# State-space scan on one core: output product by chunk with sums of squares on its diagonal, decays two chunks ahead

## What is computed

```python
xn = _rmsnorm(x, norm_w, eps)                 # x: layer-normed tokens
zxbcdt = einsum('bld,ed->ble', xn, W_in)      # z 256, x|B|C 256+32+32, dt 8
xBC = silu(causal convolution of 4 taps over tokens + conv_b)
dt = softplus(dt + dt_bias); dA = exp(dt * -exp(A_log))
state = state * dA_t + (dt_t * x_t) B_t       # for every token, 8 heads of 32 x 32
y_t = state C_t
y = y + Dp * xs
y = _rmsnorm(y * silu(z), gnorm_w, 1e-05)     # mean over the 256 channels of y
return x + einsum('ble,de->bld', y, W_out)
```

## Time and profile before

| | us |
|---|---|
| median of 3 runs | 1113.69 |
| lowest and highest of them | 1113.39, 1123.93 |
| the profiled execution's own time | 1116.23 |
| its span, first to last instruction | 1114.4 |

### The profile page before, as it was taken

How to read it: one execution, slowest core, us unless ns; L and a number is a source line. 1 busy time by engine, 2 the same in 40 slices (tenths; PEclk the granted TensorE clock), 3 DMA queues, 4 the chain that set the end, 5 groups by cost and what they waited for, 6 DMA issues and landing times.

```text
span 1114.4 us, 20011 instructions
## 1 busy us (share of the span) xinstructions
PE 928.4 (83%) x7790; PEld 737.3 (66%) x7790; DVE 712.2 (64%) x1838; ACT 542.2 (49%) x859; POOL 236.8 (21%) x194
## 2 busy tenths in 40 slices
PE   3798899988986786878787797778979999999998
PEld 2554665556655575766676676667757878888877
DVE  2856776777662746364646446564566888878875
ACT  1534554444744653628273454626334455655453
POOL 0052001110104241414223141412532001111000
PEclk8899999999986778788878778787959999999999
DMA  5420000000002200203030200303010000000000
GB/s 148 153 114 19 19 20 2 19 20 20 1 9 57 49 19 15 52 2 65 1 67 1 47 20 8 60 1 66 7 53 1 20 1 20 20 20 20 20 1 39
DMA packets 30765, 36.16 MB, mean 32 GB/s; under 512 B 4560, under 2 KB 24784, under 8 KB 30672
## 3 DMA queue, kind: packets, MB, share of 16 engines
q1 hardware_dynamic: 29520, 30.68, 11.3%
q10 hardware_dynamic: 1152, 4.19, 1.0%
...
## 4 chain that ended last, share of the span: by engine, by line
PE 53%; DVE 28%; ACT 8%; issue 6%; POOL 2%; DMA 1%; SPq 1%; DVEq 0%; ACTq 0%; POOLq 0%
PE ps L1028 6%; DVE cacc L1682 6%; PE ps L684 5%; PE ps L947 4%; PE ps L763 3%; DVE acc L1959 3%; PE ps L765 3%; PE ps L764 3%; PE ps L671 3%; DVE nmax L1539 2%; PE ps L638 2%; ACT X L1234 2%; ACT un L1354 2%; PE ps L883 2%; PE ps L643 2%
## 5 line engine op out<-in xcount | busy, mean ns | idle before, releaser
L1773 DVE SCALAR_TENSOR_TENSOR dcy<-dcy,g_sb 128x1024 f32<-128x1024 f32 x64 | 95.4, 1491 | 117.9 <-ACT dcy L1310 117.5
L1959 DVE SCALAR_TENSOR_TENSOR acc<-ps,comb,acc 128x128 f32<-128x128 f32 x512 | 141.2, 344 | 21.5 <-PE ps L1028 20.6
L1028 PEld LDWEIGHTS ps<-w_f,hid 128*128 128x128 f32 x1024 | 131.2, 191 | 16.5 <-ACT hid L1373 8.2
L1028 PE MATMUL ps<-w_f,hid 128*128 128x128 f32 x1024 | 136.7, 277 | 4.8 <-ACT hid L1373 4.8
L1373 ACT ACTIVATE hid<-ps,b_f 128x512 f32<-128x512 f32 x128 | 86.3, 686 | 107.7 <-PE ps L765 107.4
L1310 ACT ACTIVATE dcy<-ps 128x1024 f32<-128x1024 f32 x64 | 65.4, 1021 | 134.9 <-PE ps L883 134.8
L1539 DVE TENSOR_REDUCE nmax<-ps 128x1 f32<-128x1024 f32 x64 | 78.1, 1221 | 39.7 <-PE ps L643 39.3
L518 POOL TENSOR_TENSOR xdt<-xs,dts 128x256 f32<-128x256 f32 x64 | 58.3, 913 | 211.6 <-PE ps L924 211.6
L1682 DVE SCALAR_TENSOR_TENSOR cacc<-ps,cw,cacc 128x1023 f32<-128x1023 f32 (+5 forms) x72 | 91.8, 1276 | 8.6 <-ACT cacc L1247 7.2
L1163 ACT ACTIVATE probs<-ps,nmax 128x1024 f32<-128x1024 f32 x64 | 71.3, 1114 | 41.3 <-DVE nmax L1539 38.4
L671 PEld LDWEIGHTS ps<-id_f,probs 128*128 128x128 f32 x512 | 60.0, 144 | 32.5 <-issue 22.9
...
## 6 DMA issues: line engine op xcount, KB each, us to landing
...
```

The lines of the kernel that those rows point to most:

```text
L1028: last = nc.tensor.matmul(ps[:, Y_BANKS[n], t * P:(t + 1) * P], hid[n % 2][:, t * P:(t + 1) * P], w2_f[:, e, :], start=True, stop=True)
L1773: nc.vector.scalar_tensor_tensor(mix[c % 2][:], dcy[c % 2][:], 1.0, g_sb[u][:, c:c + 1, :].to_broadcast([P, NH, P]), ALU.min, ALU.mult).th ...
L1959: done = nc.vector.scalar_tensor_tensor(acc[u][:, tt, :], ps[:, bank, t * P:(t + 1) * P], comb[u][:, tt, e:e + 1], acc[u][:, tt, :], ALU.m ...
```

## The change

- **Output by chunk.** `y_t` becomes `y_w`, four blocks of gated y for each half of the channels with `w_out` as a fifth. `out_product(n)` takes a chunk's y as the stationary operand and y and `w_out` together as the moving one: 2 products of 256 columns. Half of the result is y times y transposed, whose diagonal holds the sums of squares, and half is the output. It stands in the free half of bank 6 or 7. `square`, `sum_of_squares` and `sqt` are gone. n counts chunks over all sequences.
- `mean_square(n)` on DVE multiplies the 128 x 128 half with `id_mean` (the identity divided by 256) and adds up each row into `sve`. POOL's `root` then takes one column for each chunk, and DVE's `output(n)` adds one chunk. Chunk n's product and mean stand two chunks later, its output three.
- **Decays two chunks ahead.** `dcy` has three buffers; `decay(n+2)`, `decays(n+2)` and `mixed(n+1)` stand at the head of chunk n, before the pieces.
- **Silus of x first.** `silus` starts with `cacc`, then ACT itself issues the four transfers to `c_rep` that SP issued before, then come the silus of z, g = 1 before g = 0.
- The gate products of g = 1 stand at slot 0 and wait for `m_conv_ready`, no longer for the output. Most other pieces stand 0.5 to 1.25 slots earlier. POOL's `decayed` and `weighted` are cut in halves at slots 3.5, 4.5, 5.5 and 6.5.
- Before the scan `inner_products(0, 0)` moves behind `steps(1, 1)` and the first group of products.

```diff
-        dcy = [msb(f"dcy{u}", [P, NH, P]) for u in range(2)]
+        dcy = [msb(f"dcy{k}", [P, NH, P]) for k in range(3)]
...
-            def sum_of_squares(b, c):
-                pe.wait_ge(m_square_ready, NT * b + c + 1)
+            def out_product(n):
+                k = n % 4
                 for g in range(2):
-                    last = nc.tensor.matmul(ps[:, 6 + c % 2, DI + c // 2:DI + c // 2 + 1], sqt[:, c % 4, g, :], ones_f[:, 0:1],
-                                            start=(g == 0), stop=(g == 1))
...
-            def out_product(b):
-                pe.wait_ge(m_gated_ready, NT * b + NT)
-                if b + 2 < B:
-                    pe.wait_ge(m_conv_ready, 3 * (b + 2) + 3)
...
+                    nc.tensor.matmul(ps[:, 6 + n % 2, DI:BANK].rearrange("p (k t) -> p k t", k=2), y_w[:, g, k, :],
+                                            y_w[:, g, k:5:4 - k, :], start=(g == 0), stop=(g == 1))
...
             def scan(b, u, first, last):
                 for c in range(NT):
+                    n = NT * b + c
+                    if n + 2 < NT * B:
+                        decay(n + 2)
                     pieces(b, c - 0.25)
-                    if c + 1 < NT:
-                        decay(b, u, c + 1)
                     pieces(b, c)
...
+                    if n >= 4:
+                        pe.wait_ge(m_out_added, n - 3)
+                    if n >= 2:
+                        pe.wait_ge(m_gated_ready, n - 1)
+                        out_product(n - 2)
                     output_rows(b, u, c)
...
-            pe_parts = [(cumulate, (), 1, -0.25), (gates, (0, 0), 1, 0.5), (gates, (0, 1), 1, 0.5),
-                        (gates, (1, 0), 1, 1.5), (gates, (1, 1), 1, 1.5), (turn_x, (0,), 1, 2.5),
-                        (turn_x, (1,), 1, 2.5), (turn_b, (), 1, 3), (inner_products, (), 1, 3.5),
-                        (turn_normed, (), 2, 4), (steps, (), 2, 5), (group, (0, 0), 2, 5), (group, (0, 1), 2, 5),
...
+            pe_parts = [(cumulate, (), 1, -0.25), (gates, (1, 0), 1, 0), (gates, (1, 1), 1, 0), (gates, (0, 0), 1, 0.5),
+                        (gates, (0, 1), 1, 0.5), (turn_x, (0,), 1, 2), (turn_x, (1,), 1, 2), (turn_b, (), 1, 2.5),
+                        (inner_products, (), 1, 2.5), (turn_normed, (), 2, 3), (steps, (), 2, 4),
+                        (group, (0, 0), 2, 4), (group, (0, 1), 2, 4), (group, (1, 0), 2, 4.5),
...
             def silus(b, u):
+                act.wait_ge(m_silu_ready, 3 * b + 3)
...
+                for h in range(4):
+                    nc.scalar.dma_start(c_rep[h * DS:(h + 1) * DS], cacc[b % 3][DS:2 * DS, 2, :]).then_inc(m_c_spread, 16)
+                for g in (1, 0):
+                    act.wait_ge(m_z_product, 3 * b + 3 - g)
+                    nc.scalar.activation(two(zs[u][:, g, :]), gate_banks(b, g), ACT.Silu).then_inc(m_z_ready, 1)
...
+            def decays(n):
+                act.wait_ge(m_decay_product, n + 1)
+                if n >= 3:
+                    act.wait_ge(m_y_product, n - 2)
...
+            def mean_square(n):
+                if n >= 4:
+                    dve.wait_ge(m_rms_ready, n - 3)
+                nc.vector.scalar_tensor_tensor(gram[:], ps[:, 6 + n % 2, DI:DI + P], GN2_EPS * DI, id_mean[:], ALU.add,
+                                               ALU.mult, accum_out=sve[:, n % 4:n % 4 + 1]).then_inc(m_square_mean_ready, 1)
+            def output(n):
+                dve.wait_ge(m_rms_ready, n + 1)
...
+                nc.vector.scalar_tensor_tensor(xb, ps[:, 6 + n % 2, BANK - P:BANK], srs[:, n % 4:n % 4 + 1], xb,
+                                               ALU.mult, ALU.add).then_inc(m_out_added, 1)
...
+            pool_parts = [(totals, (), 3.5), (decayed, (0,), 3.5), (decayed, (1,), 4.5), (weighted, (0,), 5.5),
+                          (weighted, (1,), 6.5)]
```

More of the change, by code:

```diff
@@ L531, in decayed, with weighted @@
                                           totals.to_broadcast([P, DS, NT - 2])).then_inc(m_decf_ready, 1)
+            def decayed(b, u, g):
                 pool.wait_ge(m_decf_ready, 2 * b + 2)
                 pool.wait_ge(m_c_spread, 64 * (b + 1))
-                for g in range(2):
-                    rows = c_dec[u][:, 1:NT, g, :]
-                    nc.gpsimd.tensor_tensor(rows, rows, c_rep[:, P:N].rearrange("p (c t) -> p c t", t=P),
-                                            ALU.mult).then_inc(m_c_decayed, 1)
-            def weighted(b, u):
+                rows = c_dec[u][:, 1:NT, g, :]
+                nc.gpsimd.tensor_tensor(rows, rows, c_rep[:, P:N].rearrange("p (c t) -> p c t", t=P),
+                                        ALU.mult).then_inc(m_c_decayed, 1)
+            def weighted(b, u, part):
                 pool.wait_ge(m_wend_ready, b + 1)
@@ L563, in attend, with pieces @@
                     norms(b - 1)
[L565 to L575 removed]
+            pool_parts = [(totals, (), 3.5), (decayed, (0,), 3.5), (decayed, (1,), 4.5), (weighted, (0,), 5.5),
+                          (weighted, (1,), 6.5)]
+            def pieces(b, slot):
+                for part, of, at in pool_parts:
+                    if slot_of(b, at) == slot and b + 1 < B:
+                        part(b + 1, (b + 1) % 2, *of)
             def scan(b, u, first, last):
                 for c in range(NT):
[L579 removed]
+                    n = NT * b + c
                     if c + 1 < NT:
                         operand(b, u, c + 1)
[L582 removed]
+                    if n >= 2:
+                        root(n - 2)
+                    pieces(b, c + 0.5)
+                    if first and c == 2:
+                        norms(B - 1)
                     if c == NT - 1 and not last:
@@ L872, in inner_products, with decay @@
                 last.then_inc(m_inner_product, 1)
-            def decay(b, u, c, first=False):
+            def decay(n):
+                b, c, u = n // NT, n % NT, n // NT % 2
                 if c == 0:
                     pe.wait_ge(m_rows_read, 64 * (b + 1))
-                    if first:
-                        pe.wait_ge(m_dt_copied, 2)
-                if not (first and c == 0):
-                    pe.wait_ge(m_decay_ready, NT * b + c)
+                if n == 0:
+                    pe.wait_ge(m_dt_copied, 2)
+                else:
+                    pe.wait_ge(m_decay_ready, n)
                 for h in range(2):
@@ L1258, in silus @@
                 for g in range(2):
-                    act.wait_ge(m_z_product, 3 * b + 2 + g)
-                    nc.scalar.activation(two(zs[u][:, g, :]), gate_banks(b, g), ACT.Silu).then_inc(m_z_ready, 1)
-                for g in range(2):
                     act.wait_ge(m_conv_ready, 3 * b + g + 1)
@@ L1333, in scan @@
                         gate_exponentials(0)
[L1337 to L1339 removed]
+            act_parts = [(factors, (), 1, 0), (silus, (), 1, 0.5), (normed, (), 2, 2), (gather_x, (), 1, 2),
+                         (gather_b, (), 1, 2.5), (high, (), 2, 3), (shortcut, (), 1, 3.5), (steps, (), 2, 4),
+                         (tap, (0,), 2, 4), (tap, (1,), 2, 4.5), (softplus, (), 2, 5), (tap, (2,), 2, 6)]
             def pieces(b, slot):
@@ L1816, in scan @@
                 for c in range(NT):
-                    if c == 0:
-                        mixed(b, u, 0)
-                        if not first:
-                            mean_square(b - 1)
+                    n = NT * b + c
                     if first:
@@ L1823, in scan @@
                     pieces(b, c - 0.25)
-                    if c < NT - 1:
-                        mixed(b, u, c + 1)
-                    if c == 1 and not first:
-                        output(b - 1, 1 - u)
+                    if n + 1 < NT * B:
+                        mixed(n + 1)
+                    if n >= 3:
+                        output(n - 3)
                     if first:
@@ L2000, in _ @@
             fronts[1]["softplus"](1)
+            mixed(0)
             scanned(dve, scan)
-            mean_square(B - 1)
-            output(B - 1, 1)
+            output(NT * B - 3)
+            for n in (NT * B - 2, NT * B - 1):
+                dve.wait_ge(m_tail_product, n - NT * B + 3)
+                mean_square(n)
+                output(n)
             scanned(dve, experts)
```

220 lines of the change are left out of this document (83 added, 137 removed).

## The result

| | median, us | ratio to before | 95% interval |
|---|---|---|---|
| changed kernel, 4 runs | 1079.61 | 0.9675 | 0.9616 to 0.9733 |
| the same once more (e5), 6 runs | 1076.5 | 0.9627 | 0.9595 to 0.9659 |

The kernel is faster by 3 to 4%. The predicted 1069 lies 11 us under the median and the range holds it. The profiled execution took 1075.48 us (span 1073.4) where that of before took 1116.23: -40.75 us, while the medians differ by 33.9 (before is 1113.54 here, with a fourth run). In the larger set of e5 they differ by 41.1 (1117.57 and 1076.5), so the profile is no outlier. I set sizes against the profile, as the prediction did.

What follows compares the result with a forecast made beforehand. PE was taken to lead 46.5 us of a 63.1 us turn, DVE 16.6. At -5.9 a turn the scan gave 32.5, with -4 before it and -8.5 at the end: together -45, so 1069 us, range 1038 to 1102.

Steps and rivals of the forecast that it cites:

- part 5: PE's decay and y of chunk 5 run while DVE works on chunk 4, through the look-ahead: -2.3 us a turn.
- part 9: DVE's mixes slow down beside POOL's c_dec and xw where DVE leads: 3 x 1.0 = +3.0 us a turn.
- Parts 1 to 3: On PE, per turn: old output product and squares leave, -9.3; product by chunk arrives, +5.0; wait for output leaves, -2.9 us.
- Part 4: PE's wait for xl shrinks from 3.04 to 1.4 us: -1.6 us a turn.
- Part 6: PE's half-clock stretch after the wait for the output goes: -3.0 us a turn, between 0 and -5.
- half clock once a turn for the most part: Sign expected in the profile after: PE's clock at half mostly once in each turn.
- Part 7: ACT's longer chain in chunks 0 to 2 delays chunk 3's exponential and PE behind it: +0.9 us a turn.
- Part 8: DVE carries more mixes, outputs and means where it leads: +4.3 us a turn, far end +7.9.
- Mixes over 2 us beside `xw`: Sign expected in the profile after: DVE's mixes take over 2 us beside POOL's xw.
- The ends: Before the scan, c_rep wait and inner_products behind other work, -4 us; from sequence 6 on, less output work, -8.5 us.
- the clock staying up with POOL out of the way: Rival: PE's clock stays up and POOL does not collide, 5.5 us more a turn, 1036 us; chance 0.20.
- the third rival: PE's clock stays down after longer waits and the kernel is slower, 1141 us at 25 us more half clock; chance 0.08.

Runs made afterwards that it cites:

- e9: Changed kernel with all but the output product by chunk (and the third buffer) put back: old slot tables, silus of z first, c_rep from SP, decays one ahead; 0.9789.
- e8: Changed kernel with exponents and their exponentials one chunk ahead again instead of two; ratio to before 0.9657.
- e2: Changed kernel with the fill: 20 products of 384 columns, results unused, in PE's gap ahead of the sums from sequence 2 on; ratio to before 0.9638.
- e11: e7 with both halves of POOL's xw at slot 2.5 and gather_x ahead of normed on ACT; 1030.34 us, ratio to before 0.9216.
- e1: Changed kernel with the four c_rep transfers issued by SP again, behind the c_dec spreads; ratio to before 0.9556.
- e3: Changed kernel with both edits of e1 and e2: c_rep from SP behind c_dec, and 20 products in PE's gap; ratio to before 0.9674.
- e6: Changed kernel with the four c_rep transfers issued by SP ahead of the c_dec spreads; ratio to before 0.9545.
- e7: e6 with the 20 products of e2 in PE's gap; ratio to before 0.9510.
- e4: Changed kernel with the pass that makes a chunk's mean done three times, two results unread; ratio to before 0.9805.
- e10: Changed kernel with both halves of POOL's xw at slot 2.5 instead of 5.5 and 6.5; ratio to before 0.9551.

## Why the prediction was right, by its own steps

The sum of a turn was -5.9 and the profile has -5.7 (63.1 to 57.4); the total was -45 and came out at -41. Its first steps carried it, and several that did not hold cancelled: part 5 gave 1.7 us less than forecast and the new wait for `X` cost 1.4, while part 9, taken as DVE's busy time, came out over 4 us better. That the turn agrees to 0.2 us is luck.

*Parts 1 to 3, right.* They sum to -7.2 a turn; less their share of DVE's added work e9 was expected at -4 to -5, and its turn is 4.2 us shorter, in an execution under e9's median. The wait for `output` is gone, and the wait for the convolution is 4.62 us (5 forecast). The new product takes 0.87 us from its start to the next product's at full clock (571.09 us) and 1.70 at half (549.88), for 0.85 and 1.6 forecast. Missed was its own wait for `X` of an earlier chunk: 10.9 us in the whole run, 1.6 in five of the six turns.

*Part 4, right.* xl: 1.4 forecast, 1.23 measured.

*Part 5, wrong.* "y of chunk 5 gets cover", -2.3. e8 shows 0.6 a turn for the look-ahead, and `mixed` one ahead was nothing new inside a sequence. The step failed in putting the cover down to the look-ahead: y(4) to y(5) takes 6.4 us in e8 and in e5, but 9.8 in e9 and 10.0 before. So it was the slot tables (or ACT's new order, which came with them in e8) that shortened that stretch; I take it that they spread the group products, which no run shows by itself. y(4) comes later in return, 36.0 us after the head in e5 instead of 31.0 in e9.

*Part 6, size right, meaning not.* Half clock fell from 22.8 to 14.7 us a turn, 8.1 x 0.48 = 3.9 where 3.0 was forecast. But e2 had another 3.4 us less at half (12.1 in e5, 8.7 in e2) and no time came back: the clock is worth what PE's chain is worth there. Only behind e11's other edits did the fill pay 0.7%. The sign "half clock once a turn for the most part" did not come: the turn from 547.02 has it around its head, again at 561.82 for 3.41 us, and at its end from 602.78.

*Part 7, mis-sized, then harmless in a turn.* The wait for the exponential was 2.00 us instead of the 0.5 that my count gave (11.8 against 11.3), since the four issues took 3.38 us on ACT's queue, not 2.44. Its mean of 1.8 us comes close to the 2 us that I had named as a sign of being wrong. e1 showed that the turn does not pay for them, as `c_rep` and `gather_x` are just behind; the start does. There the prediction had -4 and the profile -1.7. From DVE's first copy to `ein` to the head of sequence 0's scan it is 49.0 us before, 46.2 to 47.6 in the five kernels that issue `c_rep` from ACT (six executions), and 43.4 to 44.8 in e1, e3, e6 and e7 with the issues on SP.

*Part 8, right.* 0.28 + 0.08 us against 0.30; its price on the turn by e4 as assumed.

*Part 9, wrong in place and sign.* +3.0 for mixes beside POOL. The mixes took 84.1 us in the run; before, 64 of them at a mean of 1491 ns took 95.4: 1.4 us less a sequence. POOL's products came to lie beside convolutions instead, whose passes stayed at 1.27 us. In each of the first six scans only one mix lay beside half of `c_dec`, at 1.58 us; three in the scan of sequence 6 took 2.1 to 2.7. "Mixes over 2 us beside `xw`" came once. A pass that I had not counted paid: `dtw`, 1.33 us beside `xw` and 0.20 without. The Trainium skill, SBUF — State Buffer, section "Who interferes with whom", has a second half that I had left out: it names `tensor_scalar` among the passes that can take the ports shared with GpSimd, and with these numbers the trace agrees.

*The ends.* -4 and -8.5 forecast, -1.7 and -5.6 measured. In the tail the last two chunks run mean, root, addition one after the other from 801.32 us on, 6 us to the first `hid`, and POOL's products stood in DVE's way before that (e10: -4.6, its cause not tested).

Of the rivals, the clock staying up with POOL out of the way (1036) is the one that the experiments built: e11, at 1030. It needed two more edits than that rival had in mind, `c_rep` from SP ahead of `c_dec` and `gather_x` ahead of `normed`, so the nearness of the numbers is no support for that rival's working. In the third rival, 5.9 and 2 are called 7.5 together; that is the -45 over six turns, and nothing else hangs on it.
